# Seven batches of x + b summed in DRAM by accumulating transfers, and one fixed split of the rho products, in a two-layer graph kernel

## The reference

```python
def L0(h, adj, ...):                       # block attention in blocks of 64 nodes, then an MLP
    Whc = (h @ W).reshape(B, C, k, Fd)
    scores = softmax(diagonal_blocks(adj) * leaky(Whc @ a, 0.2)[..., :, None])
    out = einsum('bcij,bcjf->bcif', scores, Whc)
    y = leaky(leaky(out @ W1 + b1, .01) @ W2 + b2, .01) @ W3 + b3
    return layernorm(y + out) * ln_g + ln_b
def L1(nf, adjacency, ...):                # attention over all nodes, 4 heads of 32
    h = (nf @ W_proj.T).reshape(B, N, H, dh)
    s = leaky_relu(s_left[:, :, None] + s_right[:, None] + adjacency[..., None] * we, 0.2)
    attn = softmax(s + (-9e15) * (adjacency <= 1e-5), axis=2)
    return leaky_relu(nf + einsum('bijh,bjhd->bihd', attn, h) + bias, 0.5)
x = layernorm(x + L0(x, adj, ...))
x = layernorm(x + L1(x, adj, ...))
```

## Time and profile before

| | before |
|---|---|
| median of three runs | 1982.88 us (1981.89 to 1983.13) |
| the profiled execution | 1981.11 us |
| its span, first to last instruction | 1979.2 us |
| busy: POOL | 1866.3 us, 94% |
| busy: DVE | 1821.9 us, 92% |
| busy: PE | 1795.4 us, 91% |
| busy: ACT | 1646.4 us, 83% |
| DMA engines, mean share | 31.8% by the kernel's queue |

### The profile page before, as it was taken

One profiled execution on the slowest core, in us unless ns is written; L12 is line 12 of the kernel. 1 busy time (PEld: TensorE's weight loads), 2 busy tenths in 40 slices (PEclk: granted clock), 3 DMA queues, 4 the chain that ended last, 5 costly groups with the idle time before them and its releaser, 6 DMA issues.

```text
span 1979.2 us, 34310 instructions
## 1 busy us (share of the span) xinstructions
PE 1795.4 (91%) x11080; PEld 875.2 (44%) x11080; DVE 1821.9 (92%) x3413; ACT 1646.4 (83%) x3895; POOL 1866.3 (94%) x663
## 2 busy tenths in 40 slices
PE   7799999999999999899999999999999999878885
PEld 6544444444444444445444444444444444333332
DVE  3699999999999999999999999999999999999997
ACT  6788887899888898888988889888887898676674
POOL 3599999999999999999999999999999999999995
PEclk9899999999999999999999999999999999999999
DMA  3232315233243243333233331333315233333310
GB/s 100 73 115 91 102 50 157 83 114 106 66 138 99 81 120 100 94 113 99 79 120 100 86 119 58 121 121 91 102 54 156 81 113 91 102 96 96 102 54 11
DMA packets 138090, 190.63 MB, mean 96 GB/s; under 512 B 22328, under 2 KB 56504, under 8 KB 137912
## 3 DMA queue, kind: packets, MB, share of 16 engines
q1 hardware_dynamic: 137912, 188.44, 31.8%
HBM read 179.77 MB, written 8.65 MB: 95 GB/s over the span
## 4 chain that ended last, share of the span: by engine, by line
POOL 28%; ACT 20%; PE 19%; issue 17%; DVE 15%; SPq 0%; DMA 0%; ACTq 0%; DVEq 0%; POOLq 0%
POOL X L501 26%; PE psum L1217 15%; DVE X L1102 11%; ACT E L773 4%; PE psum L1396 3%; ACT psum L776 3%; ACT pen L734 3%; ACT squares L642 2%; DVE X L1091 2%; POOL haug L484 1%; ACT blk L590 1%; ACT blk L563 1%; ACT x1s L670 1%; ACT o_sb L670 0%; ACT act_T L563 0%
## 5 line engine op out<-in xcount | busy, mean ns | idle before, releaser
L501 POOL TENSOR_TENSOR X<-RHO,E 128x1536 f32<-128x1536 f32 (+1 forms) x512 | 1779.3, 3506 | 41.8 <-ACT E L773 35.3
L1102 DVE SCALAR_TENSOR_TENSOR X<-psum,s_j,X 128x512 f32<-128x512 f32 x2048 | 1397.4, 741 | 78.8 <-POOL X L501 68.0
L1217 PE MATMUL psum<-X,haug 128*33 128x512 f32 x4096 | 978.6, 598 | 8.2 <-ACT accU L752 4.6
L1396 PEld LDWEIGHTS psum<-ident,adj_sb 128*128 128x128 f32 x2048 | 285.9, 140 | 561.8 <-DVE X L1102 429.1
L1396 PE MATMUL psum<-ident,adj_sb 128*128 128x128 f32 x2048 | 430.6, 291 | 101.3 <-DVE X L1102 97.7
L773 ACT ACTIVATE E<-psum,we_s 128x512 f32<-128x512 f32 x512 | 395.5, 772 | 139.0 <-PE psum L1217 137.1
L1217 PEld LDWEIGHTS psum<-X,haug 128*33 128x33 f32 x4096 | 195.0, 110 | 431.7 <-issue 390.6
L776 ACT ACTIVATE psum<-psum,we_s 128x512 f32<-128x512 f32 x512 | 380.7, 744 | 0.0
L1217 PE MATMUL psum<-sgn_ident,pen 128*128 128x128 bf16 x2048 | 374.7, 219 | 0.0
L734 ACT ACTIVATE pen<-adj_sb,pen_bias 128x512 bf16<-128x512 f32 x512 | 366.8, 717 | 1.0 <-PE psum L1217 0.2
L1091 DVE TENSOR_TENSOR X<-psum,E 128x512 f32<-128x512 f32 x496 | 334.0, 673 | 3.6 <-ACT RHO L563 2.2
(11 more groups left out here) (231 smaller groups left out, 1547.5 us busy)
## 6 DMA issues: line engine op xcount, KB each, us to landing
adj_sb<-in_adj_dram SPq DMA_DIRECT2D x128, 1024.0 KB, 5.2
RHO<-rho_scratch SPq DMA_DIRECT2D x31, 1024.0 KB, 9.7
out_dram<-o_sb SPq DMA_DIRECT2D x32, 256.0 KB, 2.3
xg<-in_x_dram SPq DMA_DIRECT2D x28, 256.0 KB, 5.3
blk<-in_adj_dram SPq DMA_DIRECT2D x56, 64.0 KB, 5.1
X<-in_x_dram SPq DMA_DIRECT2D x2, 256.0 KB, 3.0
W_sb<-in_L_gnn_W_dram SPq DMA_DIRECT2D x4, 64.0 KB, 2.1
X<-in_adj_dram SPq DMA_DIRECT2D x4, 64.0 KB, 2.8
```

The source lines that it names most:

```text
L501: Q.tensor_tensor(X[m % NX][:, 0:heads, :], RHO[:, g % 2, 0:heads, :], bc(E[m % NE][:], 1, [P, heads, GROUP]), ALU.mult).then_inc(B_pool, 1)
L1102: ins = V.scalar_tensor_tensor(slot[:, h, :], TA[m % NT], s[:, k, h:h + 1], slot[:, h, :], ALU.mult, ALU.max)
L1217: return T.matmul(o, l, r, start=start, stop=stop)
L1396: T.matmul(o, adj_sb[c][:, t, at:at + P], ident[:], is_transpose=True, start=True, stop=False)
```

## The change

There is a new tensor in DRAM, `xb_d`, for `x + b` of all batches. SP fills its first batch with `ln_b` (one transfer with a row of 512 bytes repeated 2048 times), waits for that, and copies this to the seven others. POOL then issues seven transfers, one for each of the batches 1 to 7, which add `x` to what is there. They stand between the first and the second piece of `haug` of batch 0, ahead of tile 0. `chain_xb` on POOL stays for the six groups of the prologue; for the other 26 groups SP loads `xb` from `xb_d` (`load_xb`), after the batch's accumulating transfer and after the residual two groups back. `FOUR` is empty: POOL has three heads in all 512 tiles, DVE one. Most tables have some entries one or two tiles away from before; `haug` goes from (58, 59, 62, 65) to (58, 58, 61, 64). This is the core of the diff; of the tables a few lines stand for all.

```diff
-    FOUR = (11, 29)
+    FOUR = ()
-    AT_SP = {"load": (-30, -23, -3, 9)}
+    AT_SP = {"load": (-30, -23, -3, 9), "xb": (-27, -18, 5, 24)}
-    AT_DVE = {"max": (-20, -13, 12, 26), "rin": (-18, -6, 16, 27), "res": (1, 19, 30, 42)}
-    AT_POOL = {"xb": (-24, -8, 20, 25), "r_shift": (5, 24, 39, 45), "haug": (58, 59, 62, 65)}
+    AT_DVE = {"max": (-20, -13, 11, 24), "rin": (-16, -6, 17, 27), "res": (0, 19, 30, 42)}
+    AT_POOL = {"r_shift": (5, 21, 39, 48), "haug": (58, 58, 61, 64)}
+    xb_d = nc.dram_tensor("xb_scratch", [B, N, D], fp32).ap()
+    xb_g = xb_d.rearrange("b (g t p) f -> (b g) p t f", p=P, t=GT)
...
                     sp.wait_ge(xT_ps, prev(c) + 1)
-                    sp.wait_ge(xb_sb, prev(c) + 1)
+                    if c < NB + 4:
+                        sp.wait_ge(xb_sb, prev(c) + 1)
...
+            def fill(nb):
+                if nb == 0:
+                    sp.dma_start(xb_d[0], ln_b.partition_broadcast(N)).then_inc(b_filled[0], 16)
+                    sp.wait_ge(b_filled[0], 16)
+                else:
+                    sp.dma_start(xb_d[nb], xb_d[0]).then_inc(b_filled[nb], 16)
+
+            def load_xb(c):
+                s = set_of(c)
+                sp.wait_ge(xb_made[c // NB - 1], 16)
+                wait_r(sp, prev(c))
+                sp.dma_start(xb[s], xb_g[c]).then_inc(xb_in[s], 16)
...
             load_adj(0, 0)
             load_adj(0, 1)
+            for nb in range(B):
+                fill(nb)
             sp.wait_ge(prep_act, 5)
...
+            def batch_xb(nb):
+                pool.wait_ge(b_filled[nb], 16)
+                Q.dma_start(xb_d[nb], x[nb], accum_op=ALU.add, max_dma_last_dim=8192).then_inc(xb_made[nb - 1], 16)
...
-                        if n == AT_POOL["xb"][u] and m >= 0:
-                            chain_xb(c)
...
-            for q in range(NC_):
+            make_haug(0, 0)
+            for nb in range(1, B):
+                batch_xb(nb)
+            for q in range(1, NC_):
                 make_haug(0, q)
...
-                dve.wait_ge(xb_sb, c + 1)
+                if c < NB + 2:
+                    dve.wait_ge(xb_sb, c + 1)
+                else:
+                    dve.wait_ge(xb_in[s], 16 * (uses(c) - 1))
```

More of the change, by code:

```diff
@@ L42, in build_program @@
     U = range(NB)
-    FOUR = (11, 29)
-    AT_SP = {"load": (-30, -23, -3, 9)}
-    AT_PE = {"xT": (-26, -20, 0, 18), "wh0": (-26, -17, 0, 18), "wh1": (-24, -16, 5, 19), "ST": (-11, 7, 20, 29),
[3 rows of a table removed]
-    AT_ACT = {"xT": (-24, -16, 2, 20), "wh0": (-23, -15, 6, 21), "wh1": (-21, -13, 9, 22),
-          "logits": (-21, -13, 9, 25), "exp": (-19, -10, 13, 27), "soft": (-15, -5, 19, 30), "ST": (-8, 12, 23, 32),
-          "oT": (-7, 13, 24, 34), "y1": (-6, 14, 25, 35), "y2": (-5, 14, 27, 36), "ssq": (-2, 17, 28, 39),
-          "z_rstd": (0, 19, 28, 39), "r_rstd": (3, 22, 37, 44), "r_norm": (6, 24, 40, 49), "x1T": (7, 29, 46, 50),
-          "h0": (10, 29, 46, 52), "h1": (13, 31, 48, 52)}
-    AT_DVE = {"max": (-20, -13, 12, 26), "rin": (-18, -6, 16, 27), "res": (1, 19, 30, 42)}
-    AT_POOL = {"xb": (-24, -8, 20, 25), "r_shift": (5, 24, 39, 45), "haug": (58, 59, 62, 65)}
-    ONCE_PE = {"rmT": 52, "Rb": 53, "rhoT": 55, "hsum": 56}
-    ONCE_ACT = {"diag": 55, "factors": 57, "rho": 58, "hcol": 61}
+    FOUR = ()
+    AT_SP = {"load": (-30, -23, -3, 9), "xb": (-27, -18, 5, 24)}
+    AT_PE = {"xT": (-27, -20, 0, 18), "wh0": (-26, -17, 0, 18), "wh1": (-24, -15, 6, 19), "ST": (-11, 7, 20, 30),
[3 rows of a table added]
+    AT_ACT = {"xT": (-24, -18, 2, 20), "wh0": (-23, -15, 7, 21), "wh1": (-21, -13, 9, 22),
+          "logits": (-21, -13, 9, 24), "exp": (-19, -10, 13, 27), "soft": (-14, -5, 19, 28), "ST": (-8, 11, 23, 33),
+          "oT": (-7, 13, 24, 35), "y1": (-6, 14, 25, 35), "y2": (-5, 14, 26, 36), "ssq": (-3, 17, 28, 39),
+          "z_rstd": (0, 18, 29, 39), "r_rstd": (4, 21, 37, 44), "r_norm": (6, 22, 40, 49), "x1T": (9, 28, 44, 51),
+          "h0": (11, 29, 46, 52), "h1": (13, 31, 49, 52)}
+    AT_DVE = {"max": (-20, -13, 11, 24), "rin": (-16, -6, 17, 27), "res": (0, 19, 30, 42)}
+    AT_POOL = {"r_shift": (5, 21, 39, 48), "haug": (58, 58, 61, 64)}
+    ONCE_PE = {"rmT": 52, "Rb": 53, "rhoT": 55, "hsum": 57}
+    ONCE_ACT = {"diag": 55, "factors": 57, "rho": 58, "hcol": 60}
     ONCE_DVE = {"rm": 52, "R4": 54, "lam": 55}
-    ONCE_SP = {"rho": 49}
+    ONCE_SP = {"rho": 51}
     EPI_PE = {"back0": 2, "back1": 3}
@@ L66, in build_program @@
     EPI_DVE = {"part0": 4, "part1": 5, "lky": 6}
-    EPI_POOL = {"shift": 15}
+    EPI_POOL = {"shift": 12}
     EPI_SP = {"store": 15, "rho": 8}
     rho_d = nc.dram_tensor("rho_scratch", [B, H * JT, P], fp32).ap()
+    xb_d = nc.dram_tensor("xb_scratch", [B, N, D], fp32).ap()
+    xb_g = xb_d.rearrange("b (g t p) f -> (b g) p t f", p=P, t=GT)
     x_g = x.rearrange("b (g t p) f -> (b g) p t f", p=P, t=GT)
@@ L263, in build_program @@
         xb_sb = sem("xb_sb")
+        b_filled = [sem(f"b_filled{r}") for r in range(B)]
+        xb_made = [sem(f"xb_made{r}") for r in range(1, B)]
+        xb_in = [sem(f"xb_in{v}") for v in range(2)]
         exb_sb = sem("exb_sb")
@@ L451, in _ @@
                             load_chain(NB * nb + u)
+                        if n == AT_SP["xb"][u] and NB * nb + u >= NB + 2:
+                            load_xb(NB * nb + u)
                     if n == ONCE_SP["rho"]:
@@ L463, in chain_xb @@
                 pool.wait_ge(x_in[set_of(c)], 48 * uses(c))
-                if c >= NB + 2:
-                    wait_r(pool, prev(c))
                 Q.tensor_tensor(xb[s], xg[s], bc(b_bc[:], 1, [P, GT, D]), ALU.add).then_inc(xb_sb, 1)
+            def batch_xb(nb):
+                pool.wait_ge(b_filled[nb], 16)
+                Q.dma_start(xb_d[nb], x[nb], accum_op=ALU.add, max_dma_last_dim=8192).then_inc(xb_made[nb - 1], 16)
             def r_shift(c):
```

## The result

The changed kernel takes 2005.51 us (median of 4 runs, 2004.92 to 2005.79), the kernel before 1983.01 us (4 runs, 1981.89 to 1984.71). The ratio is 1.0117, 95% interval 1.0105 to 1.0129. The forecast was 1953.5 us, with a range of 1936 to 1980.

The account below looks back on a forecast made before the run. POOL, in lockstep with DVE, was taken to bound a body, with DVE the bound after the change. From 1981.1 us, less 34.4 in the loop, plus 5 at the start: 1951.7, or 1953.5 as median; range 1936 to 1980.

Parts of the forecast that it names:

- The start: Ahead of tile 0: fills nearly free, seven issues on POOL partly covered by idle time and slack; 5 us later.
- Eight of them from 30 us on end at 72 us.: Prologue: eight 1 MB DRAM-to-DRAM moves at 5.2 us per MB, ending about when POOL needs the first copy, 71.1 us.
- No wait, or a few microseconds: Prologue: POOL's wait for the copies before its accumulating transfers; a few microseconds only if the copies are slower.
- In the loop, SP and DMA: 26 `xb` loads of 256 KB on SP; the `RHO` load behind the first has cover until about 120 us; cost nothing.
- the issues hold POOL: Rival at the start: POOL held until each transfer lands, or fills late; up to 45 us, 1991 us in all; chance 0.1.
- The term for the issues: POOL ahead of tile 0: seven issues of accumulating transfers at 1.1 us each, 7.7 us, of which 3.1 covered.
- The loop: Bodies of 237.2 us shorten by 4.9 each in six, 3.5 in the seventh, 1.5 in the last: 34.4 us together.
- the step from 7.9 us down to 5.1 by a lead of POOL: DVE's idle time per body: 7.9 us remain, or 5.1 if POOL's lead hides late `E`; gain 3.5 or 6.3, middle taken.
- Middle and upper end: Gain of a body in the loop: 4.9 us as the middle, 6.3 if the new bound idles only 5.1 us.
- I give the new tables no value of their own: Loop order tables: steps move by a tile or two, only what reaching the middle gain of 4.9 us takes.
- faster by more: Whole kernel faster by more than the 0.2%, 4 us, that a measurement can tell from no change; chance given as 0.84.
- The rival of the lockstep: Loop: DVE and POOL swap as bound, idle time about 10 us, body 236 us, 1978 us in all; chance 0.15.

Follow-up runs that it names:

- e_noacc: The changed kernel without the seven accumulating transfers, all fills kept (x left out of the residual of batches 1 to 7): 1969.5 us, ratio 0.9939.
- v_oldtab: `v_spread` with the order tables of the kernel before, only the `xb` loads added, three heads on POOL everywhere: 1967.41 us, ratio 0.9931.
- v_spread: The changed kernel with fills stored from SBUF and accumulating transfers spread, one in the prologue and one per body at tile 12: 1963.25 us, ratio 0.9909.

## Why the prediction was wrong, point by point

**The start is the step that failed.** It stood at +5 us with ends of 0 and 12, and measured +41. Three statements in it:

- "Eight of them from 30 us on end at 72 us." The first took 35.0 us, from 23 to 58, and the seven copies landed between 64 and 86. The rate was taken as half of that of an adjacency load, for a transfer whose source is one row read over and over, and no row of the trace bore on that. The copies, with distinct rows, took about 4 us per MB (28 us for seven with other traffic), better than the 5.2 assumed. So the price was right for seven transfers out of eight.
- "No wait, or a few microseconds." POOL waited 10.3 us. The first fill is worth 16 us at tile 3.
- The room in the DMA engines ahead of tile 3 was counted for the fills, but the seven accumulating transfers were priced by their issue alone. Their 7 MB are 50 us of nearly full DMA engines (70 to 122 us, one landing every 5.7 us), at a time in which the prologue depends on a chain of small transfers, `rho` and the next chain's loads. This has no term in the sum at all. Its nearest sentence is "In the loop, SP and DMA", "I cost it at nothing; without the cover it costs what the transfer lands late": it looked at the `RHO` load behind the first `xb` load and not at what SP issues from 70 us on. It is worth 34.5 us at tile 3 by `e_noacc`, 25.5 where the fill is quick.

The rival *the issues hold POOL* had the right sign and place. Its other condition, that the fills come late, did come, with 10.3 us of waits. Its main one didn't: it wanted over 5.4 us an issue and 0.80 were measured. The term for the issues, 7.7 us, was too large: seven of them back to back keep POOL for 3.9.

**The loop was mis-sized.** The sums of work were right to 0.2 us: POOL 224.8 (225.0 forecast), DVE 225.9 (225.8). The gain of a body was 2.7 us, and its forecast 4.9, with a lower end of 3.5. The step that failed is the idle time, above all the step from 7.9 us down to 5.1 by a lead of POOL, of which the forecast took half. Even the 7.9 was exceeded: 234.51 less 225.90 is 8.6 us. Of DVE's waits in the body of the changed kernel:

```profile
DVE X L1133 <- POOL X L528: 5.7, 11, 1.1
DVE rden L1071 <- PE psum L1248: 1.1, 3, 0.6
DVE lky L1091 <- ACT psum L786: 0.3, 1, 0.3
```

The waits of 1.7 and 2.0 us in the four-head tiles are gone, as forecast. For POOL 5.7 us remain here and 3.7 to 5.1 in the four bodies beside it, where 4.7 were to stay (2.7 at `haug`, 2.0 behind a late `E`): the inventory of the waits was about right, that of 1.0 us behind the adds too, by the shifts above. The lead wasn't. Middle and upper end were argued from POOL building up a lead once it has less work than DVE. What it gained in time it waited: its waits for `E` rose from 4.3 to 5.7 us, and 2.9 for `rstd` came in.

"I give the new tables no value of their own": they are worth 4.2 us with the adds gone, by `v_oldtab` and `v_spread`. One sum of the prediction is off by a hundredth: its chances for "faster by more" make 0.85, not 0.84.

**The rival of the lockstep** asked for a body of 236 us with 10 us of idle time and had 0.15. The body came out at 234.5, between it and the forecast, and its reasons (DVE and POOL change places, three engines close together) describe the loop better than the forecast's. The sign that the prediction gave for it, waits for `E` of over 8 us a body, is seen only with the tables of before (8.2 and 8.7 us).

Without the start's failure the loop's own gain, 16.3 us, would have given 1966.7 plus the 5 forecast for the start, 1972: inside the range, and far from its centre. `v_spread`, with no loss at the start, is at 1963.

## What to carry to other kernels

A transfer that is "issued ahead and waited for late" still occupies the DMA engines while it runs: before placing megabytes next to a chain of small transfers, count the bytes against the rate in that stretch, and spread them over the loop, where a third of the DMA time is in use. Before a design change, try the part that costs one line; here the even split alone gave 14.3 us. When a run takes work out and puts other work in, even 0.8 us of it, compare it tile by tile before calling the first worth nothing: here an issue behind a four-head tile hid most of what the adds gave. And a busy share of 98% doesn't say that a us less on that engine is a us less of the body: price work by what ends the waits downstream, and test it by leaving a little work out on each engine.
